# Transposed one-hots of the attention round: one VectorE operation of eight tiles, or four of two tiles each

## The chip, the cores and the metric

The kernel runs on one core of one Trainium2 chip. The metric is the device time of one launch in microseconds, from runs on the chip. Times of single instructions come from one profiled execution.

## What is computed

A graph of 6250 nodes with 128 features and 106250 edges (100000 drawn ones and one loop for each node) goes through four layers, each with a residual and a layer norm. The change lies in the second one, the attention layer. Cut to what matters:

```
h = (x @ lin_w.T).reshape(n, HEADS, HEAD_DIM)
a_src = (h * att_src).sum(-1)
a_dst = (h * att_dst).sum(-1)
logits = jax.nn.leaky_relu(a_src[src] + a_dst[dst], NEG_SLOPE)
seg_max = jax.ops.segment_max(logits, dst, num_segments=n)
e = jnp.exp(logits - seg_max[dst])
denom = jax.ops.segment_sum(e, dst, num_segments=n)
alpha = e / denom[dst]
agg = jax.ops.segment_sum(h[src] * alpha[:, :, None], dst, num_segments=n)
```

The edges are sorted by destination. The logits of the edge's own destination, `a_dst[dst]`, and of its loop are looked up by a matmul: a one-hot of the destination, turned (node by edge), against 128 rows of node logits.

## The kernel before

The edges lie in 832 tiles of 128, in 104 batches of G = 8 tiles. The attention round walks through the 104 batches. Each engine has its own program, written out by hand, with semaphores between them; no scheduler moves anything. Every engine runs the body of one batch (`slot`) four times in a loop, so a lap is four batches or 32 tiles; the first and the last batches stand outside the loop.

What each engine does for a batch:

- **POOL** gathers the rows of `table_gat` (features and source logits of each edge's source) with eight indirect DMAs, line 849, one for each tile, into a ring of four buffers (tile names `H` and `GB` in the trace). It waits for the list of indices (ACT, line 1197) and for the messages of four batches earlier (line 2319).
- **DVE** starts the slot with the running maxima of the batch (lines 2328 and 2330), which wait for PE's turned logits (line 1575); then come the differences (2307, 2309), the ends of the tiles (2336), and **`ahead`, line 2258: the turned one-hots of the next batch**, one `tensor_scalar` over 128 x 1024 bf16 elements: `LROW` holds the local destination of each edge in every partition, and it is compared with the partition's number `pidx`. Behind it on DVE stand the messages (2316 and four operations in 2319), the scans across tiles (2341 to 2352), the adding of sums (1969, 1971), more scans (2359 to 2370) with two additions for the looked-up logits (2269), and last the next batch's edge logits, `edge_sum` (line 2288), which wait for the gather of that batch, with 2295 and 2302 behind them.
- **PE** does a small matmul for the ends (1618), the eight look-up matmuls of the next batch (1585), which wait for the whole of `ahead`, the sums of an earlier batch (1599, 1600), small matmuls for maxima and scale (1626, which waits for 2344; 1629, 1630), the eight matmuls that sum the messages (1635), which wait for 2319, and then the transposes 1640 and 1575. DVE's next slot waits for 1575.
- **ACT** makes exponentials (1173, 1176), stages indices (1197), copies the looked-up logits (1192), and makes the straight one-hots (1183, 1186).
- **SP** loads the next `LROW` (line 754) when `ahead` of two batches earlier is through, and other inputs of the batch.

The constant `PIECE` is 2; the messages (2319) are already cut by it: one operation for every two tiles.

Of the kernel before, what the change touches and what calls it, by code (L numbers as in the profile page):

```python
# [22 lines left out]
ALU = mybir.AluOpType  # L23
# [3 lines left out]
P = 128  # L27
# [12 lines left out]
G = 8  # L40
# [29 lines left out]
PIECE = 2  # L70
# [12 lines left out]
def build(nc, a, out):  # L83
    ctx = ExitStack()
    with ctx:
        ctx.enter_context(nc.allow_non_contiguous_dma(reason="columns of indices and of biases, once"))

        def sb(name, shape, dt=FP32):
            return ctx.enter_context(nc.sbuf_tensor(name, shape, dt))

        def sem(name):
            return ctx.enter_context(nc.semaphore(name))
# [25 lines left out]
        pidx = sb("pidx", [P, 1])  # L118
# [82 lines left out]
        def of_tout(columns):  # L201
            free_t[0] += columns
            return TOUT[:, :, :].rearrange("p b n -> p (b n)")[:, free_t[0] - columns:free_t[0]]

        MW = of_tout(2 * G * MW_COLS).rearrange("p (b j f) -> p b j f", b=2, j=G)
        LROW = of_tout(G * P).bitcast(BF16).rearrange("p (b e) -> p b e", b=2)
        OHT = of_tout(G * P // 2).bitcast(BF16).rearrange("p (j e) -> p j e", j=G)
# [77 lines left out]
        def blocks_of(g):  # L285

            return range(4 * g, min(4 * g + 4, XBLOCKS))
# [242 lines left out]
        def n0_centered(g, n):  # L530

            return PS[:, 4 * (g % 2) + n // 2, n % 2 * (NL + P):(n % 2 + 1) * (NL + P)]
# [28 lines left out]
        chain_d, soft_d, ahead_d = sem("chain_d"), sem("soft_d"), sem("ahead_d")  # L561
# [11 lines left out]
        def at(steps, k, step="all"):  # L573

            return (k + BEFORE) * len(steps) + (steps.index(step) + 1)
# [1282 lines left out]
        def _(dve):  # L1858
# [362 lines left out]
            for g in range(GROUPS):  # L2221
# [9 lines left out]
                for n, q in enumerate(blocks):  # L2231
                    ins = dve.scalar_tensor_tensor(X[:, q * P:(q + 1) * P], n0_centered(g, n)[:, NL:], inv_root[:, q:q + 1], BC,
                                                   ALU.mult, ALU.add)
# [20 lines left out]
            def ahead(k, b, at_i):  # L2254

                dve.wait_ge(lrow_in[b], 16 * at_i)
                dve.wait_ge(look_p, at(ONE, k - 1))
                dve.tensor_scalar(OHT[:, :, :].rearrange("p j e -> p (j e)"), LROW[:, b, :], pidx[:, 0:1], None,
                                  ALU.is_equal).then_inc(ahead_d, 1)

            def look_part(k, b, n):

# [127 lines left out]
            def slot(i, c):  # L2390
# [10 lines left out]
                if now < BATCHES - 1:  # L2401
                    ahead(k + 1, 1 - b, half + 1 + b)
# [30 lines left out]
            def next_edges(k, c, at_i):  # L2433
# [3 lines left out]
                edge_or_loop(k, c % 2)  # L2437

            ahead(0, 0, 1)
            for n in (1, 2):  # L2440
                look_part(0, 0, n)
# [10 lines left out]
            for t in STEPS:  # L2452
                g = t
                if 0 <= g < GROUPS:
                    m, b = len(blocks_of(g)), g % 2
# [25 lines left out]
                if 0 <= g < GROUPS:  # L2481
# [5 lines left out]
                    for n, q in enumerate(blocks):  # L2487
                        row = X[:, q * P:(q + 1) * P]
                        ins = dve.scalar_tensor_tensor(row, ZB[g % 2][:, n, P:2 * P], inv_root[:, q:q + 1], row, ALU.mult, ALU.add)
# [349 lines left out]
```

## Time and profile before

| | |
|---|---|
| median of three runs | 5758.0 us (5751.86 to 5763.01) |
| the profiled execution, whole | 5760.18 us |
| its span, first to last instruction | 5758.3 us |
| the attention round's batches in it (line 2328) | 104, from 2470 to 3526 us |
| mean granted TensorE clock of the span | 0.839 |

Times in the trace are microseconds from the span's start. "Idle before" is the time an engine stood still ahead of an instruction, and the name behind the arrow is what ended it; "issue" means that nothing shown ended it. The duration of an instruction overlaps with the next one's on the same engine, so a chain of operations is measured from start to start.

### The profile page before, as it was taken

The numbers are of one execution on the slowest core, as the hardware profiler recorded it, in microseconds if no ns is written. First come the engines' busy times: TensorE is split into PE (matmuls) and PEld (weight loads), VectorE is DVE, ScalarE is ACT, GpSimd is POOL, SyncE is SP. The second block draws the span as 40 slices with busy tenths as digits, with TensorE's granted clock in tenths as the row PEclk, the third lists the DMA queues.
The fourth block names the chain that finished last, engine by engine and source line by source line (L and its number), as shares of the span: only waits on it lengthen the run. The fifth ranks groups of instructions, "written<-read, shape, count | busy, mean of one in ns | idle before, by whom it ended". The sixth has DMA issues, their size and how long they took to land. (4 is left out here: it accounts for less than half of the span.)

```text
span 5758.3 us, 111258 instructions
## 1 busy us (share of the span) xinstructions
PE 4169.4 (72%) x25518; PEld 3454.7 (60%) x25519; DVE 2718.9 (47%) x10515; ACT 1818.5 (32%) x5132; POOL 3986.0 (69%) x4143
## 2 busy tenths in 40 slices
PE   4688888887777787656666668566665566886896
PEld 3577777776777776545555556454544454665664
DVE  8743333433333333256666666555555545334332
ACT  0122222222222222334444444544444442001001
POOL 3177777766777777377777775577777775776777
PEclk6699999999999999755666666888888888998998
DMA  3265656652222122133333332233333324554553
GB/s 87 48 171 153 162 153 163 157 147 60 52 52 52 52 52 52 44 88 85 87 84 87 85 86 70 74 102 101 98 99 107 104 88 142 188 178 137 189 187 111
DMA packets 380789, 609.48 MB, mean 106 GB/s; under 512 B 118627, under 2 KB 288132, under 8 KB 368516
## 3 DMA queue, kind: packets, MB, share of 16 engines
q1 hardware_dynamic: 246884, 331.68, 19.2%
q0 software_dynamic: 129024, 267.91, 18.4%
q8 instruction: 241, 3.95, 0.3%
q14 instruction: 512, 4.19, 0.2%
q10 hardware_dynamic: 4128, 1.75, 0.1%
HBM read 524.61 MB, written 76.38 MB: 104 GB/s over the span
## 5 line engine op out<-in xcount | busy, mean ns | idle before, releaser
L1477 PE MATMUL PS<-ROOM 128*128 128x128 f32 x8320 | 1046.4, 282 | 101.3 <-ACT ROOM L1065 99.8
L1477 PEld LDWEIGHTS PS<-ROOM 128*128 128x128 f32 x8320 | 989.1, 196 | 159.4 <-ACT ROOM L1065 109.3
L889 POOL DMA_INDIRECT GB<-table,IDX x832 | 801.3, 963 | 352.0 <-issue 247.8
L1065 ACT COPY ROOM<-PS 128x512 f32<-128x512 f32 x1040 | 609.4, 586 | 798.8 <-PE PS L1491 793.5
L889 POOL DMA_INDIRECT GB<-in_x,IDX x416 | 403.3, 969 | 296.8 <-ACT IDX L1040 157.0
L2148 DVE TENSOR_TENSOR ROOM<-ROOM,PS 128x128 f32 x312 | 89.7, 288 | 896.4 <-PE PS L1501 875.5
L889 POOL DMA_INDIRECT ROOM<-table,IDX x416 | 404.5, 972 | 137.5 <-issue 125.4
L849 POOL DMA_INDIRECT H<-table_gat,IDX x416 | 410.7, 987 | 126.8 <-issue 115.2
L849 POOL DMA_INDIRECT GB<-table_gat,IDX x416 | 406.0, 976 | 127.6 <-issue 125.6
L889 POOL DMA_INDIRECT H<-in_x,IDX x416 | 404.6, 973 | 126.8 <-issue 126.2
L889 POOL DMA_INDIRECT H<-table,IDX x416 | 396.8, 954 | 126.8 <-issue 122.5
L861 POOL DMA_INDIRECT GB<-table,IDX x352 | 335.0, 952 | 152.0 <-issue 105.8
L1635 PE MATMUL PS<-ROOM,OH 128*128 128x144 f32 x1664 | 428.0, 450 | 1.0 <-DVE RS L2376 1.0
L1491 PE MATMUL PS<-OH,GB 128*128 128x256 f32 (+1 forms) x1664 | 340.8, 359 | 119.6 <-DMA GB<-table,IDX 75.0
L861 POOL DMA_INDIRECT ROOM<-table,IDX x352 | 334.7, 951 | 107.3 <-issue 107.0
L1635 PEld LDWEIGHTS PS<-ROOM,OH 128*128 128x128 f32 x1664 | 395.1, 330 | 2.6 <-issue 1.0
L1491 PEld LDWEIGHTS PS<-OH,GB 128*128 128x128 f32 x1664 | 283.6, 210 | 165.3 <-issue 98.4
L1034 ACT CAST ROOM<-PS 128x550 f32 x450 | 299.1, 665 | 241.1 <-PE PS L1417 185.2
L2055 DVE SCALAR_TENSOR_TENSOR H<-iota_w,key,ROOM 128x256 f32<-128x256 f32 x416 | 173.8, 482 | 320.5 <-DVEq L2128 123.8
L1491 PE MATMUL PS<-OH,H 128*128 128x256 f32 x832 | 227.0, 434 | 95.9 <-DMA H<-in_x,IDX 55.1
L1710 PE MATMUL PS<-ROOM 128*128 128x384 bf16 x1470 | 263.4, 332 | 34.3 <-DVE ROOM L2581 33.1
L1710 PE MATMUL PS<-ROOM,PACK 128*128 128x384 bf16 x1470 | 270.6, 338 | 12.6 <-issue 11.8
(418 smaller groups left out, 7769.0 us busy)
## 6 DMA issues: line engine op xcount, KB each, us to landing
H<-one_over SPq DMA_DIRECT2D x416, 128.0 KB
ROOM<-one_over SPq DMA_DIRECT2D x416, 128.0 KB
neighbours<-ROOM SPq DMA_DIRECT2D x30, 1700.0 KB
ROOM<-neighbours SPq DMA_DIRECT2D x30, 1700.0 KB
PACK<-neighbours SPq DMA_DIRECT2D x30, 1700.0 KB
ROOM<-local_row SPq DMA_DIRECT2D x104, 256.0 KB
GB<-table,IDX POOLq DMA_INDIRECT x1184
ROOM<-table,IDX POOLq DMA_INDIRECT x768
```

The source lines that it names most:

```text
L849: pool.indirect_dma_start(out=out[:, j, :], out_offset=None, in_=r.table.dram[:, :], in_offset=bass.IndirectOffsetOnAxis(ap=idx[:, j:j + 1 ...
L861: pool.indirect_dma_start(out=RING_ROWS[c][:, j * P:(j + 1) * P], out_offset=None, in_=m.table.dram[:, :], in_offset=bass.IndirectOffsetOn ...
L889: pool.indirect_dma_start(out=r.rows[c][:, j * P:(j + 1) * P], out_offset=None, in_=r.dram[:, :], in_offset=bass.IndirectOffsetOnAxis(ap=I ...
L1034: act.copy(MADE_HALVES[:, :, :, bass.ds(offsets[n] + 1, SPAN - 1)], counted_of(2)[:, :, :, 1:SPAN])
L1065: act.copy(to.rearrange("p r (j d) -> p r j d", j=r.per), of.rearrange("p (j d r) -> p r j d", j=r.per, d=NEAR))\
L1477: ins = nc.tensor.matmul(PS[:, 4, 0:P], r.near[1 - b][:, t * P:(t + 1) * P], r.weights[:, t * P:(t + 1) * P], start=t == 0, stop=t == r.re ...
L1491: ins = nc.tensor.matmul(PS[:, n, j % r.per * r.cols:(j % r.per + 1) * r.cols], r.rows[c][:, j * P:(j + 1) * P], r.hot[b][:, j * r.cols:(j ...
L1635: ins = nc.tensor.matmul(PS[:, 1 - b, 0:MW_COLS], hot(1 - b)[:, j, :], MW[:, 1 - b, j, :], start=j == 0, stop=j == G - 1)
L1710: ins = nc.tensor.matmul(PS[:, bank, 0:3 * P], NEIGH[e][:, h, 0:P], XS[:, h, :], start=h == 0, stop=h == XBLOCKS - 1)
L2055: ins = dve.scalar_tensor_tensor(to, columns, key, WINDOWS[b][:, j * r.cols:(j + 1) * r.cols], ALU.is_equal, ALU.mult, accum_out=wstage[:, ...
L2148: dve.tensor_tensor(dst, dst, PS[:, 5, 0:P], ALU.add).then_inc(added, 1)
```

## The change

`ahead` makes the one-hots in four operations of two tiles (256 columns) in place of one of eight (1024 columns). All four write the same buffer as before; the waits stand ahead of the first and the semaphore's increment is on the last, so PE, SP and DVE itself see one event for a batch, as before. The other engines' programs are the same, and so is the order of everything else on DVE.

```diff
                 dve.wait_ge(lrow_in[b], 16 * at_i)
                 dve.wait_ge(look_p, at(ONE, k - 1))
-                dve.tensor_scalar(OHT[:, :, :].rearrange("p j e -> p (j e)"), LROW[:, b, :], pidx[:, 0:1], None,
-                                  ALU.is_equal).then_inc(ahead_d, 1)
+                for j in range(0, G, PIECE):
+                    ins = dve.tensor_scalar(OHT[:, j:j + PIECE, :].rearrange("p j e -> p (j e)"), LROW[:, b, j * P:(j + PIECE) * P],
+                                            pidx[:, 0:1], None, ALU.is_equal)
+                ins.then_inc(ahead_d, 1)
```

VectorE's stream at the start of the second slot, before (H holds the logits and scans, ROOM the one-hots and messages, V the ends of the tiles):

```order
L2328 SCALAR_TENSOR_TENSOR H<-H,PS 64x128
L2330 SCALAR_TENSOR_TENSOR H<-H 64x128
L2307 TENSOR_TENSOR SPARE<-H,PS 128x128
L2309 TENSOR_TENSOR RD<-RZ 8x1
L2336 TENSOR_TENSOR V<-jmask,H 64x16
L2258 TENSOR_SCALAR ROOM<-ROOM,pidx 128x1024
L2316 TENSOR_TENSOR ROOM<-ROOM,PACK 128x8x8
L2319 TENSOR_TENSOR ROOM<-GB,ROOM 128x2x128 x4
```

The same piece of VectorE's stream now (all its lines stand two further down in the file):

```order
L2330 SCALAR_TENSOR_TENSOR H<-H,PS 64x128
L2332 SCALAR_TENSOR_TENSOR H<-H 64x128
L2309 TENSOR_TENSOR SPARE<-H,PS 128x128
L2311 TENSOR_TENSOR RD<-RZ 8x1
L2338 TENSOR_TENSOR V<-jmask,H 64x16
L2259 TENSOR_SCALAR ROOM<-ROOM,pidx 128x256 x4
L2318 TENSOR_TENSOR ROOM<-ROOM,PACK 128x8x8
L2321 TENSOR_TENSOR ROOM<-GB,ROOM 128x2x128 x4
```

Four operations stand where one stood, ahead of the messages; nothing else has another place.

## Rows read from the trace of the kernel before

**Rows 1.** The page: busy time of each engine, and the clock by slices.
```profile
PE 4169.4 (72%) x25518; PEld 3454.7 (60%) x25519; DVE 2718.9 (47%) x10515; ACT 1818.5 (32%) x5132; POOL 3986.0 (69%) x4143
...
PEclk6699999999999999755666666888888888998998
```

**Rows 2.** Groups of POOL instructions, 2590 to 3490 us (22 laps).
```profile
line engine op names shapes xcount | busy us, mean ns | idle before us <-releasers
L849 POOL DMA_INDIRECT H<-table_gat,IDX x352 | 344.3, 978 | 107.3 <-issue 96.0 <-ACT IDX L1197 10.7 <-DVE ROOM L2319 0.6
L849 POOL DMA_INDIRECT GB<-table_gat,IDX x352 | 341.7, 971 | 107.3 <-issue 106.7 <-DVE ROOM L2319 0.3 <-ACT IDX L1197 0.3
```

**Rows 3.** Line 849 alone: shortest, median and longest gather.
```profile
L849 POOL DMA_INDIRECT GB<-table_gat,IDX x416: 940/944/2718, 2451.2 to 3497.6; - x139
```

**Rows 4.** Timeline of VectorE, one lap: edge logits (2288) and slot starts (2328).
```profile
3003.01 0.41 DVE L2328 TENSOR_TENSOR_SCAN H<-H,PS 64x128 f32<-64x128 f32 x1 [4.29 <-issue]
...
3012.49 0.41 DVE L2328 TENSOR_TENSOR_SCAN H<-H,PS 64x128 f32<-64x128 f32 x1 [2.39 <-PE PS L1575]
...
3021.36 0.41 DVE L2328 TENSOR_TENSOR_SCAN H<-H,PS 64x128 f32<-64x128 f32 x1 [1.87 <-PE PS L1575]
...
3028.55 0.23 DVE L2288 TENSOR_TENSOR H<-H 128x64 f32<-128x64 f32 x1 [0.83 <-DMA H<-table_gat,IDX]
...
3030.90 0.41 DVE L2328 TENSOR_TENSOR_SCAN H<-H,PS 64x128 f32<-64x128 f32 x1 [1.40 <-PE PS L1575]
...
3038.83 0.23 DVE L2288 TENSOR_TENSOR H<-GB,H 128x64 f32<-128x64 f32 x1 [1.78 <-DMA GB<-table_gat,IDX]
...
3043.84 0.41 DVE L2328 TENSOR_TENSOR_SCAN H<-H,PS 64x128 f32<-64x128 f32 x1 [4.06 <-issue]
```

**Rows 5.** Timeline of all engines, around line 2258 in one slot.
```profile
3013.62 0.47 DVE L2258 TENSOR_SCALAR ROOM<-ROOM,pidx 128x1024 bf16<-128x1024 bf16 x1
...
3014.04 0.23 DVE L2316 TENSOR_TENSOR ROOM<-ROOM,PACK 128x64 f32<-128x64 f32 x1
...
3014.65 0.49 PE L1585 MATMUL PS<-SPARE,ROOM 128*128 128x48 bf16 x8 [0.61 <-DVE ROOM L2258]
...
3015.79 0.18 DVE L2344 TENSOR_TENSOR_SCAN ROW_B<-H,ROW_F 8x16 f32<-8x16 f32 x1
3016.00 0.15 DVE L2349 TENSOR_TENSOR RZ<-CARRY,ROW_B 8x1 f32<-8x1 f32 x1
3016.08 0.13 DVE L2350 COPY RZ<-ROW_B 8x1 f32<-8x1 f32 x1
...
3016.12 0.36 PE L1626 MATMUL PS<-ROW_B,sel 8*64 8x16 f32 x2
```

**Rows 6.** Line 2258 alone: shortest, median, longest.
```profile
L2258 DVE TENSOR_SCALAR ROOM<-ROOM,pidx x104: 467/468/661, 2466.2 to 3513.3; 128x1024 bf16<-128x1024 bf16 x104
```

**Rows 7.** Timeline of VectorE, another round: eight comparisons in a row, 512 bytes each.
```profile
5011.92 1.66 DVE L2560 TENSOR_SCALAR OH<-iota_w,local 128x128 f32<-128x128 f32 x8 [1.54 <-DVEq L2713]
```

**Rows 8.** Lines 2560 and 2383 alone: shortest, median, longest (2383: one column).
```profile
L2560 DVE TENSOR_SCALAR OH<-iota_w,local x704: 267/281/526, 4820.3 to 5701.7; 128x128 f32<-128x128 f32 x176
L2383 DVE TENSOR_SCALAR ROOM<-ROOM,RS x104: 201/214/216, 2484.2 to 3537.6; - x104
```

**Rows 9.** Timeline of VectorE and of POOL, gathers that meet line 2258.
```profile
2554.53 0.99 POOL L849 DMA_INDIRECT GB<-table_gat,IDX  x1 [0.30 <-issue]
...
3413.40 0.47 DVE L2258 TENSOR_SCALAR ROOM<-ROOM,pidx 128x1024 bf16<-128x1024 bf16 x1
...
3413.48 1.22 POOL L849 DMA_INDIRECT GB<-table_gat,IDX  x1 [0.30 <-issue]
...
3482.66 1.12 POOL L849 DMA_INDIRECT GB<-table_gat,IDX  x1 [0.30 <-issue]
```

**Rows 10.** Windows of one lap: busy time, count, granted clock (PEclk), DMA, GB/s.
```profile
3003.00:3020.00 17.00, 12.46 (x66) 10.29 (x67) 13.05 (x64) 8.97 (x27) 13.04 (x14) 0.50 0.34 75
3020.00:3024.00 4.00, 1.73 (x18) 1.25 (x16) 2.44 (x9) 0.77 (x4) 3.09 (x4) 0.93 0.56 123
```

## The prediction

> **What bounds the kernel now.** First the page: no engine is busy all the time, POOL 69% and DVE 47% [rows 1]. A share of the span says nothing about one stage, so the next view is the stage of the change, and in it the groups of the engine that may never stand still. Over 900 us of the attention round POOL issues 704 gathers, busy 344.3 + 341.7 = 686.0 us, with an idle time of 2 x 107.3 = 214.6 us ahead of them [rows 2]. That is all of the 900 us, and the idle time is 0.305 us ahead of every gather alike, whatever releaser is named: the pause between two gathers, not a wait. POOL never waits for data here. An undisturbed gather takes 0.944 us [rows 3], so 32 of them, a lap, take 32 x (0.944 + 0.305) = 39.97 us. The lap measured is 900 / 22 = 40.9 us; the missing 0.95 us are gathers that took longer (mean 0.975 us). So the round is bound by **POOL issuing gathers**, with about 0.95 us a lap of disturbance.
>
> The second view is DVE's timeline of a lap [rows 4]. It shows how much the engine that the change loads has to spare. DVE waits for gathered rows ahead of line 2288 for 0.83 us in the third slot and for 1.78 us in the fourth; in the first two slots it does not. All slot starts but the first wait for PE's transpose 1575, which stands behind the 16 message matmuls, and these behind DVE's own work of the slot: DVE and PE form one chain, at 9.48, 8.87 and 9.54 us a slot. Ahead of the first slot of each lap DVE stands for 4.1 to 4.3 us with no releaser, at the place where its loop jumps back. The chain is therefore never shorter than 3043.84 - 3003.01 = 40.83 us less the last wait, 1.78: **39.05 us a lap** if gathers cost nothing. POOL's 40.8 lies above it by 1.78 us. The wait of the third slot is covered by PE's slot time and doesn't count beside it.
>
> **The change, part by part.** *Removed:* one operation of 0.468 us [rows 6]; the next operation starts 0.42 to 0.45 us after it (3014.04 - 3013.62) [rows 5]; I take 0.43. *Added:* four of 256 bf16 columns. The nearest rows are comparisons of the same kind (a tensor against a number per partition, both in memory) over 128 f32 columns, which are the same 512 bytes: 0.281 us each [rows 8], and eight in a row take 1.66 us [rows 7], so they start every (1.66 - 0.28) / 7 = 0.197 us. Four then hold up the next operation by 4 x 0.20 = 0.80 us in place of 0.43, **0.37 us more**, and the one-hots are ready after 3 x 0.20 + 0.27 = 0.87 us in place of 0.47, **0.40 us later**. Bounds: the same with no overlap at all, 4 x 0.28 - 0.43 = 0.69 us more; and, from below, operations of one column start every 0.08 us (3016.00, 3016.08) [rows 5], to which comes a quarter of what the large one needs for its data, (0.468 - 0.214) / 4 = 0.063 us with the one-column comparison as the fixed part [rows 6, 8]: 4 x 0.145 - 0.43 = 0.15 us more. I take 0.38 for both paths, near the row that is like it in kind and bytes, and keep 0.15 and 0.69.
>
> *Who sees these 0.38 us.* Behind `ahead` on DVE everything of the slot is later, the messages first. On PE the look-up matmuls (start 0.56 us after the one-hots are ready) and, behind them, 1626 are later too; 1626 starts within 0.15 us of the end of 2344 [rows 5], so both paths move by about the same, and I count one shift of 0.38 a slot and not two. The queue of SP gets its release 0.40 us later for a load that has a batch of time. POOL waits for the messages of four batches earlier, and these are ready ten microseconds before it asks, which is why rows 2 show no such wait; nothing of POOL's own moves. Four slots: 4 x 0.38 = 1.52 us a lap. The chain becomes 39.05 + 1.52 = 40.57 us, still under the 40.83 that this lap takes. The added work is **hidden by the wait for gathered rows**, which shrinks from 1.78 to 0.26 us; if that cover were gone, it would cost 24 x 1.52 = 36 us.
>
> *What can change POOL itself.* In rows 9 a gather starts 0.08 us after line 2258 and takes 1.22 us, 0.28 more than 0.94; 3413.48 + 0.28 = 3413.76, which is 0.11 us before the comparison ends. In the loop 37 gathers meet line 2258 in this way, the first at 2554.53 and the last at 3482.66 [rows 9], some 0.1 us each, 3.8 us in all. Others are held by line 2319 and by the scans in the same way. An operation that holds for h delays a gather that falls into it by h/2 on average, and each of 32 gathers a lap falls into it with a chance of h / 10.2 for each slot. With h of 0.29 for each of 2258 and the four of 2319 (durations less 0.13), and about 0.27 for three scans and 0.1 for five small operations, the sum of h squared is 0.084 + 0.336 + 0.22 + 0.05 = 0.69, and the delay a lap is 32 x 0.69 / (2 x 10.2) = 1.08 us, against 0.95 measured. Four pieces hold for 0.1 us each with a gap between: 0.04 in place of 0.084, so 0.07 us a lap less, 24 x 0.07 = **1.7 us less**. All later operations of a slot also move against the gathers by 0.4 to 1.5 us, so the rest is drawn anew; since laps repeat nearly alike, the draw is the same 24 times. Half of it up or down, if the meeting points change, would be 0.2 us a lap or 5 us, and downward the chain stops it at 0.26 us a lap, 24 x 0.26 = 6 us.
>
> The Trainium skill has a rule for this ("SBUF — State Buffer", "Who interferes with whom"): VectorE and GpSimd share a pair of ports, and whoever issues first keeps it for the whole instruction. By it shorter instructions give the pair back sooner; the trace agrees for rows 9. It has one against the change too ("VectorE: DVE Perf Modes", "The TRN2 errata"): each instruction with its source in SBUF pays a fixed latency, so tiles should have 512 elements or more. Its formula of 58 cycles and a quarter cycle per element makes 4 x 127 - 327 = 181 ns more for four pieces (an estimate from that page), and its measured fixed part of 150 cycles would make 469 ns more; the rows lie between, and by the first figure the sum would be a chain of 39.8 us, by the second one of 40.9.
>
> **The sum.** The loop: -1.7 us for the shorter hold, 0 for 1.52 us of hidden work a lap. The eight batches outside the loop: the start waits for a load anyway and POOL's ring is four batches deep, 0; behind the last gather no `ahead` follows, 0. Together -2 us against the profiled execution, 5760.2 - 2 = 5758.2; its time is 2.2 us above the median of the runs, so **5756 us**.
>
> **The rivals.** *The port decides (faster).* If the pieces start nearly as close as the lower bound (0.15 to 0.25 us more a slot), the chain has 0.8 us of room below 40.83, and the gathers may lose half of their disturbance: -0.48 us a lap, -11.5 us, 5746 or less. For it: rows 9 and the chain of small operations. Against it: eight comparisons at 0.197 us, and only 3.8 us of all delays are line 2258's own. 8 in 100.
>
> *DVE and PE become the bound (slower).* From 1.78 / 4 = 0.445 us a slot on, the wait for gathered rows is used up and each further bit counts four times a lap. With no overlap between pieces (0.69) the lap is 39.05 + 2.76 = 41.81 us, 0.98 more, 24 x 0.98 = +23.5 us, 5781. For it: 0.38 is close to the point. Against it: every other run of like operations on this engine overlaps. The bound of 0.2% is passed from 0.56 us a slot on. 11 in 100.
>
> *The clock.* The second slot is 0.6 us shorter than its neighbours; its message matmuls run into a stretch of full clock (0.93, against 0.50 before it) [rows 10]. Should the later matmuls miss it, the chain is 40.57 + 0.6 = 41.2 us, +0.34 a lap, +8 us, 5764. 4 in 100, within the 0.2%.
>
> *The code.* The loop's body is twelve instructions longer, and DVE already stands 4.1 to 4.3 us at each jump back [rows 4]. If a second such stop came up in the lap, it would be 40.57 + 4.1 = 44.7, +3.8 a lap, +92 us, 5848. The Trainium skill tells of that stop as a fetch of a page of code after a taken branch ("Runtime: NRT & Kernel Launch", "Instruction fetch mechanics"). For it: the stop is there. Against it: there is none inside the four slots now. 3 in 100.
>
> **How the numbers follow.** The forecast, hidden work and slightly less disturbance, has 74 in 100, and its own range is 5749 to 5765. About 0.2%, 11.5 us, is what a measurement of this kernel can tell from no change. Faster by more: 0.08, the first rival. Slower by more: 0.11 + 0.03 = 0.14. Within: 0.74 + 0.04 = 0.78. The range from 5746 to 5770 leaves out half of the first two rivals and the last one, and thin ends of the forecast.
>
> **What would show it.** Four operations of some 0.27 us that start every 0.2 us; 2316 some 0.37 us later behind 2336; the wait of line 2288 in the fourth slot down from 1.78 to 0.3 us; POOL still with 0.305 us ahead of every gather and a mean of 0.965 to 0.98 us for one. The argument is wrong if that wait is gone and POOL shows waits for line 2319 or for its indices, or if DVE stands still at a second place of the lap; if POOL's mean stays but the time moves, the cause lies outside the round.

## The result, and the profile after

The changed kernel takes 5865.97 us (median of four runs, 5858.07 to 5876.2) against 5758.76 us, a ratio of 1.0189 with a 95% interval of 1.0172 to 1.0206: **slower by 107 us**, where 5756 us was forecast. Its profiled execution has a span of 5856.2 us against 5758.3, so 97.9 us of the loss can be looked for in the traces.

The first view is the page of each kernel. First the kernel before, its groups of gathers:

```profile
L849 POOL DMA_INDIRECT H<-table_gat,IDX x416 | 410.7, 987 | 126.8 <-issue 115.2
L849 POOL DMA_INDIRECT GB<-table_gat,IDX x416 | 406.0, 976 | 127.6 <-issue 125.6
```

The page of the changed kernel, its engines and the same groups:

```profile
PE 4159.3 (71%) x25518; PEld 3444.8 (59%) x25519; DVE 2752.1 (47%) x10827; ACT 1820.9 (31%) x5132; POOL 4086.0 (70%) x4143
...
L849 POOL DMA_INDIRECT H<-table_gat,IDX x416 | 474.2, 1140 | 126.8 <-issue 124.0
L849 POOL DMA_INDIRECT GB<-table_gat,IDX x416 | 440.3, 1058 | 127.6 <-issue 118.2
```

VectorE's busy time grew by 33 us, POOL's by 100 [rows 1]. The 832 gathers of the attention round took 474.2 + 440.3 = 914.5 us in place of 816.7, **97.8 us more, which is the whole loss**; their idle time, 126.8 + 127.6, is the same to a tenth. So the profile shows no place where POOL waits longer for anything. It does the same work, and each gather lasts 118 ns longer on average. From the first gather's start to the last one's it is 1166.8 us in place of 1069.0; the stretches ahead of and behind the round did not change.

The same in the loop, the groups of POOL from 2590 to 3490 us (against [rows 2]):

```profile
L849 POOL DMA_INDIRECT H<-table_gat,IDX x320 | 364.2, 1138 | 97.5 <-issue 95.1 <-ACT IDX L1197 2.1 <-DVE ROOM L2321 0.3
L849 POOL DMA_INDIRECT GB<-table_gat,IDX x323 | 341.2, 1056 | 98.4 <-issue 91.7 <-ACT IDX L1197 6.4 <-DVE ROOM L2321 0.3
```

That is 643 gathers instead of 704, with a mean of 705.4 / 643 = 1.097 us; the pause is still 195.9 / 643 = 0.305 us. POOL is the bound as before; a lap is now 32 x 1.402 = 44.9 us.

What VectorE does at the start of a slot is as forecast. Line 2259 alone, shortest, median and longest:

```profile
L2259 DVE TENSOR_SCALAR ROOM<-ROOM,pidx x416: 267/268/468, 2470.8 to 3615.6; 128x256 bf16<-128x256 bf16 x139
```

VectorE's timeline around the pieces in one slot (start, duration, engine, line, operation):

```profile
3012.05 0.86 DVE L2259 TENSOR_SCALAR ROOM<-ROOM,pidx 128x256 bf16<-128x256 bf16 x4
3012.83 0.21 DVE L2318 TENSOR_TENSOR ROOM<-ROOM,PACK 128x64 f32<-128x64 f32 x1
3012.97 1.41 DVE L2321 TENSOR_TENSOR ROOM<-H,ROOM 128x256 f32<-128x256 f32 x4
```

POOL's timeline at the same time:

```profile
3013.46 1.74 POOL L849 DMA_INDIRECT GB<-table_gat,IDX  x1 [0.30 <-issue]
3015.50 0.94 POOL L849 DMA_INDIRECT H<-table_gat,IDX  x1 [0.30 <-issue]
```

A piece takes 0.268 us, four of them 0.86 us, and the next operation starts 0.78 us after the first. The gather that starts in the second of the four message operations takes 1.74 us, 0.80 more than the undisturbed 0.94. That brings its release, worked out as start plus excess, to 3013.46 + 0.80 = 3014.26 (its *excess* is what it takes beyond the undisturbed 0.944 us), which is 0.12 us before the *last* of the four ends (3012.97 + 1.41 = 3014.38). In the kernel before, a gather that came in the same way was let in at the end of the one operation that it met. VectorE's timeline there:

```profile
3004.13 0.47 DVE L2258 TENSOR_SCALAR ROOM<-ROOM,pidx 128x1024 bf16<-128x1024 bf16 x1
3004.58 0.23 DVE L2316 TENSOR_TENSOR ROOM<-ROOM,PACK 128x64 f32<-128x64 f32 x1
3004.73 1.43 DVE L2319 TENSOR_TENSOR ROOM<-H,ROOM 128x256 f32<-128x256 f32 x4
```

And POOL's, still of the kernel before:

```profile
3005.10 1.20 POOL L849 DMA_INDIRECT GB<-table_gat,IDX  x1 [0.30 <-issue]
```

Start plus excess is 3005.36, some 0.13 us before the second message operation ends; two more followed it without a gap, and they held nothing. I worked this out for every gather of both traces. Start plus excess falls close to "end of some VectorE operation less 0.12 to 0.13 us" (0.19 us for the scans) for nearly all. "Held by" counts the VectorE operations from the one that the gather met to the one at whose end it was let in:

```
                        before            after
sum of all excess       31.9 us           129.7 us
held by one operation   171:  23.1 us     111:  16.0 us
held by 2 to 5 in a row   3:   2.6 us      70:  61.6 us
held by 6 or more         3:   5.4 us      24:  48.5 us
not attributed            6:   0.4 us      11:   3.2 us
over 600 ns               6 gathers       74 gathers, 101.5 us
```

In the changed kernel 110 us of excess are gathers held by a **row of operations instead of one**, against 8.0 us before; that difference is the loss. The longest ones met the pieces: the gather at 3031.51 started as the pieces did and was let in when the messages ended, nine operations later. VectorE's timeline in that slot of the changed kernel:

```profile
3031.54 0.86 DVE L2259 TENSOR_SCALAR ROOM<-ROOM,pidx 128x256 bf16<-128x256 bf16 x4
3032.32 0.21 DVE L2318 TENSOR_TENSOR ROOM<-ROOM,PACK 128x64 f32<-128x64 f32 x1
3032.46 1.41 DVE L2321 TENSOR_TENSOR ROOM<-GB,ROOM 128x256 f32<-128x256 f32 x4
```

POOL's:

```profile
3031.51 3.18 POOL L849 DMA_INDIRECT H<-table_gat,IDX  x1 [0.30 <-issue]
```

**What differs ahead of such a row.** The message operations are the same in both kernels and start 0.335 us apart in both. Two things of the moment at which they start differ. VectorE's sequencer, which reads its program and does the waiting, can be ahead of the engine. How far it has come shows in the register load of line 596, which the sequencer does itself and which stands in the stream just behind the four messages. That load in the slot above of the kernel before (line 596 alone; its start stands twice, to a tenth):

```profile
L596 DVEq TENSOR_LOAD <-meta x1: 750/750/750, 3004.9 to 3004.9; - x1
```

And in the slot of the changed kernel:

```profile
L596 DVEq TENSOR_LOAD <-meta x1: 756/756/756, 3012.8 to 3012.8; - x1
```

Before, the load starts 0.14 us *after* the first message operation (3004.73); after, 0.2 us *before* it (3012.97): the sequencer had handed over all four and gone on. What holds the sequencer back is the wait for the exponentials that stands ahead of line 2318 (2316 before); they come from line 1173 of ScalarE. Its timeline in the slot of the kernel before:

```profile
3004.09 0.31 ACT L1173 ACTIVATE ROOM<-SPARE 128x128 f32<-128x128 f32 x1 [5.04 <-DVE SPARE L2307]
```

And of the changed kernel:

```profile
3012.00 0.31 ACT L1173 ACTIVATE ROOM<-SPARE 128x128 f32<-128x128 f32 x1 [5.14 <-DVE SPARE L2309]
```

They end about 0.27 us after the comparison's start in both kernels (3004.40 against 3004.13, 3012.31 against 3012.05). One large comparison then has 0.2 us left to run, four pieces have 0.6. In the first case the sequencer is released just in time, in the second with time to spare. The other difference is that line 2318 starts 0.07 us before the operation ahead of it has ended, where line 2316 did so by 0.02 us in the slot shown, and that it is shorter. Its duration (shortest, median, longest) in the kernel before, as line 2316:

```profile
L2316 DVE TENSOR_TENSOR ROOM<-ROOM,PACK x104: 204/224/300, 2477.5 to 3535.3; 128x64 f32<-128x64 f32 x104
```

And in the changed kernel, as line 2318:

```profile
L2318 DVE TENSOR_TENSOR ROOM<-ROOM,PACK x104: 200/206/228, 2482.9 to 3637.1; 128x64 f32<-128x64 f32 x104
```

The median of this operation, 224 or 206 ns, turned out to be the quickest sign of which case a kernel is in.

Lastly VectorE's waits in the loop (engine, line, what it waited for: sum, times, longest), of the kernel before:

```profile
DVE H L2288 <- DMA GB<-table_gat,IDX: 38.8, 22, 2.3
DVE H L2288 <- DMA H<-table_gat,IDX: 20.1, 23, 1.5
```

And of the changed kernel:

```profile
DVE H L2290 <- DMA H<-table_gat,IDX: 93.1, 39, 3.6
DVE H L2330 <- issue: 72.0, 20, 4.2
...
DVE H L2290 <- DMA GB<-table_gat,IDX: 58.3, 24, 3.6
```

It waits for gathered rows for 151.4 us in place of 58.9. The added work did not use the wait up; POOL became slower and made it longer. The stop without a releaser still comes once a lap, 3.6 us on average, and at no second place.

### The profile page after: what moved, and what is told of

It is laid out like the page before. It is cut to its first block and busy times, and to the rows that moved or that the text cites. A ratio compares the mean times of both kernels' runs of the same rounds, so it can differ in the third digit from the quotient of the medians.

```text
span 5856.2 us, 111570 instructions
## 1 busy us (share of the span) xinstructions
PE 4159.3 (71%) x25518; PEld 3444.8 (59%) x25519; DVE 2752.1 (47%) x10827; ACT 1820.9 (31%) x5132; POOL 4086.0 (70%) x4143
## 5 line engine op out<-in xcount | busy, mean ns | idle before, releaser
L849 POOL DMA_INDIRECT H<-table_gat,IDX x416 | 474.2, 1140 | 126.8 <-issue 124.0
L849 POOL DMA_INDIRECT GB<-table_gat,IDX x416 | 440.3, 1058 | 127.6 <-issue 118.2
L889 POOL DMA_INDIRECT H<-in_x,IDX x416 | 404.7, 973 | 126.8 <-issue 126.5
L889 POOL DMA_INDIRECT H<-table,IDX x416 | 396.4, 953 | 126.8 <-issue 121.3
```

What stands on the lines that cost most here:

```text
L849: pool.indirect_dma_start(out=out[:, j, :], out_offset=None, in_=r.table.dram[:, :], in_offset=bass.IndirectOffsetOnAxis(ap=idx[:, j:j + 1 ...
L889: pool.indirect_dma_start(out=r.rows[c][:, j * P:(j + 1) * P], out_offset=None, in_=r.dram[:, :], in_offset=bass.IndirectOffsetOnAxis(ap=I ...
```

## The experiments

The theory: **VectorE operations that the sequencer hands over ahead of their start keep GpSimd out from the first to the last, as if they were one instruction; operations that it hands over one at a time let GpSimd in at each end.** The rivals: the messages' later start by itself (they meet the gathers elsewhere, or VectorE and TensorE become the bound), and the pieces by themselves. The results together; "line 2316" is the first message operation under whatever number it has:

```
kernel                                ratio to before [95%]    excess  >600 ns  line 2316
                                                               of all           median
before                                                         31.9 us    6      224 ns
after                                 1.0189 [1.0172, 1.0206]  129.7     74      206
e1  after, wait for pieces            0.9996 [0.9986, 1.0005]   29.7      1      225
e2  before, wait for comparison       0.9981 [0.9971, 0.9991]   25.1      0      226
e2b the same kernel, more runs        0.9994 [0.9985, 1.0003]   25.1      0      226
e3  before, filler behind comparison  1.0086 [1.0069, 1.0103]   84.9     64      203
e7  before, filler earlier            1.0018 [1.0009, 1.0028]   41.5      6      225
e5  before, wait between messages     1.0050 [1.0033, 1.0067]   21.4      1      225
e4  two pieces of four                1.0088 [1.0070, 1.0106]   91.0     50      206
e8  four pieces, wait on third        1.0021 [1.0012, 1.0030]   37.2      7      225
e9  two pieces, wait on first         0.9991 [0.9981, 1.0000]   29.0      4      225
e10 messages as one operation         1.0045 [1.0029, 1.0060]   55.3     25      224
```

**e1: the changed kernel, with nothing but a wait for the last piece ahead of the messages.** VectorE does more waiting and the messages start later still.

```diff
                 if now < BATCHES - 1:
                     ahead(k + 1, 1 - b, half + 1 + b)
+                    ahead_own(k + 1, "oht")
                 if 1 <= now <= BATCHES:
                     messages(k - 1, (c + 3) % 4)
```

> The changed kernel, and behind the four pieces VectorE waits for their own end before it goes on to the messages. Theory A (one long hold): back-to-back operations keep the shared ports from POOL as one block; the pieces start so close that they join with 2318 and 2321 into one block of 2.2 us, and a gather that meets it takes up to 3.2 us. The wait cuts the block in two (some 0.7 and 1.4 us), so gathers over 2.5 us vanish and the time falls most of the way back, to 5760 to 5790. Theory B (lateness): the 0.37 us by which everything of the slot is later moves the gathers into the messages, whatever stands ahead of them; with the wait the slot is later still, and the time stays at 5840 or more.

Measured: 5756.85 us, ratio 0.9996 (0.9986 to 1.0005). The whole loss is gone. VectorE's timeline of a slot:

```profile
3011.33 0.86 DVE L2259 TENSOR_SCALAR ROOM<-ROOM,pidx 128x256 bf16<-128x256 bf16 x4
3012.45 0.23 DVE L2318 TENSOR_TENSOR ROOM<-ROOM,PACK 128x64 f32<-128x64 f32 x1 [0.26 <-DVE ROOM L2259]
```

POOL's groups from 2590 to 3490 us:

```profile
L849 POOL DMA_INDIRECT H<-table_gat,IDX x352 | 352.1, 1000 | 107.3 <-issue 102.1 <-DVE ROOM L2321 4.9 <-ACT IDX L1197 0.3
L849 POOL DMA_INDIRECT GB<-table_gat,IDX x351 | 334.0, 951 | 107.0 <-issue 100.9 <-ACT IDX L1197 6.1
```

Line 2318 starts 1.12 us after the first piece, 0.34 later than in the changed kernel, and yet the gathers are back at 686.1 / 703 = 0.976 us. That speaks against both rivals at once: the pieces are all there and the messages are later than ever. It came out 3 us below the 5760 to 5790 of the theory. The pieces by themselves still form a short row here: 25 gathers were held across two to four of them, 9.5 us in all, and the longest excess is 0.75 us. The run also shows the cover of the prediction at work: in this trace VectorE has no wait for gathered rows left in the loop, and the time is that of the kernel before.

**e3: the kernel before, with a filler behind the comparison.** Two reductions of a constant into a tile that nobody reads keep VectorE busy for as long as the extra pieces do. No one-hot is cut.

```diff
+        filler = sb("filler", [P, 2])
...
                 if now < BATCHES - 1:
                     ahead(k + 1, 1 - b, half + 1 + b)
+                    for n in range(2):
+                        dve.tensor_reduce(filler[:, n:n + 1], iota_f[:, :], AXIS.X, ALU.add)
```

> The kernel before, with the one whole comparison, and behind it two reductions of 128 x 128 f32 to one column (some 0.4 us together, one input, not among the operations that met gathers in the trace). They make the rest of the slot as late as the change does, but neither cut the comparison nor join it to the messages. Theory A: within 15 us of 5758. Theory B: the lateness alone does it, 5840 or more.

Measured: 5809.12 us, ratio 1.0086 (1.0069 to 1.0103), 64 gathers over 600 ns. VectorE's timeline in one slot (lines stand one higher):

```profile
2641.22 0.47 DVE L2259 TENSOR_SCALAR ROOM<-ROOM,pidx 128x1024 bf16<-128x1024 bf16 x1
2641.62 0.46 DVE L2405 TENSOR_REDUCE filler<-iota_w 128x1 f32<-128x128 f32 x2
2642.01 0.20 DVE L2317 TENSOR_TENSOR ROOM<-ROOM,PACK 128x64 f32<-128x64 f32 x1
2642.14 1.41 DVE L2320 TENSOR_TENSOR ROOM<-H,ROOM 128x256 f32<-128x256 f32 x4
```

POOL's timeline beside it:

```profile
2642.82 1.56 POOL L850 DMA_INDIRECT GB<-table_gat,IDX  x1 [0.31 <-issue]
```

The gather came in the third message operation and was let in at the end of the fourth, no sooner. So the loss comes without the changed comparison: these two reductions, which keep VectorE busy between the exponentials and the messages, are enough. The expectation was **missed** on both sides: the theory as I had it then, with the cut comparison as the cause, gave 5758 within 15 us, and lateness alone 5840 or more.

The loss is half that of the changed kernel, since the rows are shorter. The longest excess is 1.31 us, against 2.24, and the part "6 or more" (48.5 us) is missing. The reductions themselves hold nothing. VectorE's timeline in another slot:

```profile
2909.76 0.46 DVE L2405 TENSOR_REDUCE filler<-iota_w 128x1 f32<-128x128 f32 x2
```

POOL's:

```profile
2909.80 0.94 POOL L850 DMA_INDIRECT H<-table_gat,IDX  x1 [0.30 <-issue]
```

This gather started 0.04 us into the first reduction and was not held at all, in a slot in which the register load stands 0.21 us ahead of the first message. The same goes for all 28 that started within a reduction and 0.13 us or more before its end: their excess is at most 0.01 us. Gathers that met the comparison were let in at its end. So a row is not just anything that was handed over ahead: here it began behind the reductions.

**e7: the same filler, but ahead of the differences**, from which the exponentials are made, so that they come later too (the kernels of e7, e4, e8 and e2b ran beside a kernel before of 5764.23 us).

```diff
+                if now < BATCHES - 1:
+                    for n in range(2):
+                        dve.tensor_reduce(filler[:, n:n + 1], iota_f[:, :], AXIS.X, ALU.add)
                 if 1 <= now <= BATCHES:
                     differences(k - 1, 1 - b)
```

> The kernel before, with the same two reductions (0.4 us) as in the run with them behind the comparison, but now ahead of the differences (2307), so that the exponentials, and with them the wait ahead of the messages, are as late as all the rest. Theory C (the lead): a run of message operations keeps POOL out as one block only where the sequencer has issued all of it before its first operation begins; the traces so far show the register load behind the messages 0.2 to 0.4 us ahead of the first message operation where a block is kept, and 0.02 us or more behind it where POOL gets in between. Here the wait for the exponentials holds the sequencer back as before, so no block: 5750 to 5775. Theory B (lateness): the slot is 0.4 us later just the same, so 5800 or more.

Measured: 5774.23 us, ratio 1.0018 (1.0009 to 1.0028), 10 us. The same two operations in the same slot cost 10 us here and 49 us in e3; the place alone decides. The sequencer is held by the exponentials as before, and only 6 gathers pass 600 ns. These 10 us, too, are in gathers that lasted longer (41.5 us of excess against 31.9) and not in a wait: 15 gathers were held across short rows that end with the comparison, lines 2308, 2310, 2337 and 2259, for 7.7 us in all. Together with e1 this bounds what up to 0.7 us of later work a slot costs in this round: nothing to 10 us.

**e2 and e2b: the kernel before, with the wait of e1**, the same kernel twice, first with few runs and then with more.

```diff
                 if now < BATCHES - 1:
                     ahead(k + 1, 1 - b, half + 1 + b)
+                    ahead_own(k + 1, "oht")
```

> The kernel before with the same wait behind the whole comparison, 0.1 to 0.2 us later. Theory A: the comparison already lets POOL in before the messages, so nothing changes: 5750 to 5770. Theory B: between before and after, 5770 to 5830.

> The kernel before with the wait behind the whole comparison once more, with more rounds, since one round gave a ratio of 0.9981 (0.9971 to 0.9991). Theory C: the few blocks of the first and last batches are gone (8 us in the trace of before) and the loop is as it was, so 0.1 to 0.3% faster, 5742 to 5752.

Measured: 5747.03 us, 0.9981 (0.9971 to 0.9991), then 5762.63 us, 0.9994 (0.9985 to 1.0003). The six gathers over 600 ns (8.0 us of excess, in the first and last batches) are gone from both traces, and the excess falls from 31.9 to 25.1 us. But the gain of the first eight runs was not confirmed by eleven more, and the 5742 to 5752 us expected of these were **missed**: no difference that can be measured.

**e5: the kernel before, with a wait for its own result between the messages.** VectorE stops after each of the first three, so that a row of four can't exist.

```diff
-        SOFT_D = ("diff", "rd", "own", "m", "rs", "sums", "aux")
+        SOFT_D = ("diff", "rd", "own", "m1", "m2", "m3", "m", "rs", "sums", "aux")
...
+                    if j + PIECE < G:
+                        ins.then_inc(soft_d, 1)
+                        soft_own(k, "m%d" % (j // PIECE + 1))
```

> The kernel before, with VectorE waiting for the end of each of the first three message operations (line 2319) before the next, some 0.1 us each. Theory A: no block is longer than 0.4 us, so no gather takes over 1.4 us anywhere, also in the first and last batches (six did before, 8 us in all), and the disturbance of a lap falls from 0.95 to 0.5 us or so; VectorE's chain grows by 4 x 0.35 = 1.4 us a lap and stays hidden: 5740 to 5755. Theory B, in which only the meeting points count: anything from 5750 to 5840, with long gathers still there.

Measured: 5790.66 us, ratio 1.0050 (1.0033 to 1.0067). The excess is the smallest of all, 21.4 us, and yet the kernel is 31 us slower, where 5740 to 5755 were expected: a **miss**, and another bound. VectorE's timeline in one slot:

```profile
3020.91 1.79 DVE L2319 TENSOR_TENSOR ROOM<-H,ROOM 128x256 f32<-128x256 f32 x4
3023.30 0.23 DVE L2344 TENSOR_TENSOR_SCAN ROW_F<-H,CARRY,PS 8x16 f32<-8x16 f32 x1 [0.60 <-issue]
```

Its two largest waits in the loop:

```profile
DVE H L2331 <- PE PS L1575: 172.0, 75, 3.3
DVE ROW_F L2344 <- issue: 49.5, 84, 0.6
```

One of POOL's two groups in the loop:

```profile
L849 POOL DMA_INDIRECT H<-table_gat,IDX x342 | 329.6, 964 | 129.5 <-issue 107.7 <-DVE ROOM L2319 20.6 <-ACT IDX L1197 1.2
```

The messages take 0.36 us longer, and the register load of line 596, which before ran beside them, now comes behind them and holds up line 2344 by 0.59 us. That is about 1 us a slot. VectorE waits for TensorE (172.0 us, against 125.3 before and 70.4 in the changed kernel) and no longer for gathered rows, and POOL waits 20.6 us for messages in this group, against 0.6 in [rows 2]; over the whole round POOL is idle for 288 us in place of 254. The rival "VectorE and TensorE become the bound" exists, and this is what it looks like. In the changed kernel POOL's idle time is that of before, and VectorE waits longer for gathered rows.

**e4: two pieces of four tiles.** The extra time on VectorE is about a fifth of that of four pieces (the next operation starts 0.52 us after the first, against 0.45 in the kernel before and 0.78).

```diff
-                for j in range(0, G, PIECE):
-                    ins = dve.tensor_scalar(OHT[:, j:j + PIECE, :] ... LROW[:, b, j * P:(j + PIECE) * P],
+                for j in range(0, G, 4):
+                    ins = dve.tensor_scalar(OHT[:, j:j + 4, :] ... LROW[:, b, j * P:(j + 4) * P],
```

> Two pieces of four tiles: the next operation is held up by some 0.53 us, against 0.43 (whole) and 0.80 (four pieces). Theory C: the exponentials are ready some 0.4 us after the comparison starts, so the sequencer gets a lead of 0.1 us, less than the 0.2 us seen with kept blocks: some blocks at most, 5760 to 5800. If the number of pieces alone counted: half of the loss, 5810.

Measured: 5816.47 us, ratio 1.0088 (1.0070 to 1.0106), 50 gathers over 600 ns. I had expected so small a lead of the sequencer to be harmless, and **missed**. VectorE's timeline in one slot:

```profile
2608.37 0.59 DVE L2259 TENSOR_SCALAR ROOM<-ROOM,pidx 128x512 bf16<-128x512 bf16 x2
2608.89 0.21 DVE L2318 TENSOR_TENSOR ROOM<-ROOM,PACK 128x64 f32<-128x64 f32 x1
2609.03 1.41 DVE L2321 TENSOR_TENSOR ROOM<-GB,ROOM 128x256 f32<-128x256 f32 x4
```

POOL's:

```profile
2609.50 1.77 POOL L849 DMA_INDIRECT H<-table_gat,IDX  x1 [0.30 <-issue]
```

The row holds as in the changed kernel. The register load starts 0.02 to 0.07 us behind the first message in most of these slots, only 0.07 to 0.12 us sooner than in the kernel before, so a small difference in the lead is enough. The time is also close to the 5810 us that were expected if the number of pieces alone counted; e9, with the same two pieces, rules that out.

**e8: four pieces, and a wait for the third.** The last piece still runs when the sequencer goes on, and VectorE hardly stands still.

```diff
-        AHEAD_D = ("oht", "look1", "look2", "sum", "edge", "any")
+        AHEAD_D = ("oht3", "oht", "look1", "look2", "sum", "edge", "any")
...
+                    if j == 2 * PIECE:
+                        ins.then_inc(ahead_d, 1)
...
                     ahead(k + 1, 1 - b, half + 1 + b)
+                    ahead_own(k + 1, "oht3")
```

> The changed kernel, with VectorE waiting for the end of the third piece (not the last) before it issues the messages: the sequencer is held back, the engine itself hardly is (it still has the fourth piece to do). Theory C: the messages are issued as they begin, no block is kept, 5745 to 5765. A variant of A, in which an empty moment of the engine is what lets POOL in: there is none here, so 5840 or more.

Measured: 5775.45 us, ratio 1.0021 (1.0012 to 1.0030), 10 us above the range of the theory and 65 below that of the rival. Of 45 gathers that started in the first three messages and were held for 0.05 us or more, 43 were let in at the end of the operation that they met. So it takes no pause as long as that of e1 (0.26 us): nine tenths of the loss are gone. The 7 gathers over 600 ns (11.0 us, the longest excess 2.26 us) all lie in the first and last batches, outside the loop; four of them met the pieces and were held to the end of the messages, across the point of the wait. In the slots of these four the register load comes 0.20 us ahead of the first message, while in the loop it comes 0.13 us behind it. Of the 11 us that remain, the traces show 5.9 between the first and the last gather; the rest is not explained.

**e9: two pieces, and a wait for the first.** The edit of e8 on the kernel of e4.

```diff
-        AHEAD_D = ("oht", "look1", "look2", "sum", "edge", "any")
+        AHEAD_D = ("oht1", "oht", "look1", "look2", "sum", "edge", "any")
...
+                    if j == 0:
+                        ins.then_inc(ahead_d, 1)
...
+                    ahead_own(k + 1, "oht1")
```

> The changed kernel with two pieces of four tiles, and VectorE waits for the end of the first piece before it issues the four message operations. Without that wait the same two pieces gave 5816.5 us, with 50 gathers over 600 ns (64.1 us of excess); the run of messages had then been issued 0.04 to 0.09 us before its first operation began. Theory of the sequencer's lead (a run of message operations that was issued before its first operation starts keeps GpSimd out until the whole run ends; one that is issued operation by operation lets it in at each operation's end): the wait makes the messages be issued later than the second piece's start, so no such lead remains in most slots; fewer than 15 gathers over 600 ns, excess 25 to 45 us, 5750 to 5775 us. Rival, that two back-to-back pieces and what follows them leave GpSimd no opening whatever the sequencer did: the pieces and the messages follow each other as closely as before, so 40 gathers or more over 600 ns, 5800 to 5825 us.

Measured: 5753.09 us, ratio 0.9991 (0.9981 to 1.0000), 4 gathers over 600 ns, all outside the loop, excess 29.0 us, as the theory had it. VectorE's timeline in one slot:

```profile
3190.12 0.62 DVE L2259 TENSOR_SCALAR ROOM<-ROOM,pidx 128x512 bf16<-128x512 bf16 x2
3190.76 0.22 DVE L2320 TENSOR_TENSOR ROOM<-ROOM,PACK 128x64 f32<-128x64 f32 x1
3190.90 1.42 DVE L2323 TENSOR_TENSOR ROOM<-H,ROOM 128x256 f32<-128x256 f32 x4
```

POOL's:

```profile
3191.31 1.15 POOL L849 DMA_INDIRECT GB<-table_gat,IDX  x1 [0.30 <-issue]
```

Line 2320 starts 0.64 us after the first piece, 0.12 later than in e4, with no pause to speak of (0.02 us). The same phase of a gather, 0.41 to 0.47 us into the messages, gives 1.77 us in e4 and 1.15 us here.

**e10: the kernel before, with the four messages as one operation.** A row that holds should act like one long instruction; here is one.

```diff
-                for j in range(0, G, PIECE):
-                    tiles = slice(j, j + PIECE)
+                for j in range(0, G, G):
+                    tiles = slice(j, j + G)
...
-                                            MW[:, b, tiles, P:P + HEADS].unsqueeze(3).to_broadcast([P, PIECE, HEADS, HD]), ALU.mult)
+                                            MW[:, b, tiles, P:P + HEADS].unsqueeze(3).to_broadcast([P, G, HEADS, HD]), ALU.mult)
```

> The kernel before, with the four message operations of 256 columns each made one operation of 1024 columns, so that VectorE reads two tensors of SBUF for about 1.1 us without an end in between. Theory that a held run of four acts on GpSimd as one long operation: gathers that meet it are held up to 1.2 us more; with one such run for about eleven gathers and a hit in a third of the slots, some 60 to 100 gathers over 600 ns, an excess of 80 to 130 us against 31.9 us in the kernel before, 5800 to 5860 us. Rival, that the loss of the changed kernel comes from the pieces themselves and not from the length for which the messages keep the ports: excess stays under 45 us, 5750 to 5770 us.

Measured: 5782.33 us, ratio 1.0045 (1.0029 to 1.0060), 25 gathers over 600 ns, excess 55.3 us. VectorE's timeline in one slot:

```profile
2783.64 1.22 DVE L2319 TENSOR_TENSOR ROOM<-GB,ROOM 128x1024 f32<-128x1024 f32 x1
```

POOL's:

```profile
2784.19 1.48 POOL L849 DMA_INDIRECT H<-table_gat,IDX  x1 [0.30 <-issue]
```

Start plus excess is 2784.73, 0.13 us before the operation's end, as for a held row. The mechanism is that of the changed kernel; its size was **missed**: 80 to 130 us of excess and 5800 to 5860 us were expected. The one operation is 1.22 us long, while a held row with the pieces in it reaches 2.2 us, and the gathers happened to come late in it (95 met it, 35.4 us, a mean of 0.37 us each). VectorE does the same work in less time here, and the kernel is slower.

## Why the prediction was wrong

**The step that failed is "What can change POOL itself".** It took each VectorE operation for an obstacle of its own, so that a hold h costs h squared over two and cutting one operation into four must help: 1.7 us less. The sum of squares agreed with the trace of before (1.08 us a lap against 0.95), but only because in that trace each operation did release POOL at its end. The runs show that to be a condition of the moment. Nine operations of 0.2 to 0.4 us, the pieces and the messages, were one obstacle of up to 2.2 us in the changed kernel. By the same sum, the four messages as one obstacle of 1.41 - 0.13 = 1.28 us put 1.64 in the place of 0.336, which is 32 x 1.30 / 20.4 = 2.0 us more a lap; pieces and messages as one of 2.2 us put 4.84 in the place of 0.42, 6.9 us more. The 97.8 / 24 = 4.1 us a lap that were lost lie between: the rule that I used had the loss in it, if I had asked when neighbours count as one. "Half of it up or down" was no bound for this. None of the rivals had the mechanism.

The Trainium skill ("SBUF — State Buffer", "Who interferes with whom") says of VectorE's two-port modes that whoever issues first has the shared ports for the whole instruction, and that an operation with two inputs in SBUF contends with a GpSimd instruction that reads. The trace of e10 agrees with the second: an operation of 1.22 us with two inputs kept a gather out until 0.13 us before its end. Taken instruction by instruction, no gather that meets a message would be held for more than about 0.3 us; the trace of after has 0.80 us at 3013.46, and the measurement decides.

The other steps, in their order. *What bounds the kernel*: right, POOL issuing gathers, before and after. *The pieces' cost*: 0.20 us apart and 0.27 us long was forecast, 0.195 to 0.197 and 0.268 measured; the next operation 0.78 us behind the first against 0.80. *Hidden*: right as far as it went. e1 has 0.34 us a slot on top of the change and loses nothing. By my sum its chain would be 39.05 + 4 x 0.67 = 41.7 us, and its laps are 40.97, as before (40.98): the chain is less stiff than I had it, and the rival "VectorE and TensorE become the bound" was overrated. It begins somewhere between the 0.67 us a slot of e1, which cost nothing, and the 0.95 of e5. *The wait for gathered rows* went from 58.9 to 151.4 us and not down, since POOL itself was late; the sign that I had named for the forecast, a POOL mean of 0.965 to 0.98 us, failed with 1.097. *The code*: no second stop, as forecast. *The clock*: nothing points to it. The granted TensorE clock of the round is 0.61 in both traces, and the loss is in POOL's durations to 0.1 us.

What could have been read beforehand: the trace of the kernel before holds six gathers over 600 ns, all in the first and last batches, up to 1.86 us ([rows 3] shows a longest one of 2.718 us against a median of 0.944). I took them for odd ends. By the same reading they are held rows; in all six the register load starts 0.20 to 0.25 us ahead of the messages.

**What stays open.** Take the ten traces other than e5 and e10, and in them the 541 gathers that started within the first three messages and were held for 0.05 us or more. Where the register load started 0.125 us or more after the first message, 292 of 292 were held by no more than the operation that they met. Where it started less than 0.10 us after it, or before it, 182 were held to the end of the row and 60 were not (7 lie between the two, none held to the end). Most of the 60 share a second sign: by how much line 2316 and its like overlap the operation ahead of them. At 60 to 74 ns of overlap 176 of the 179 gathers were held to the end, at 75 to 80 ns 52 of 53 were not. What these few nanoseconds stand for the trace does not show, so early handing over is not the whole condition. Nor is it told apart from the way in which the row begins: where the sequencer hands over one at a time, line 2316 overlaps the operation ahead by less than 60 ns, or starts behind its end, in 282 of the 292. Nor does the theory say why the reductions of e3, handed over ahead like the rest, hold nothing. That the resource is the shared pair of ports was not tested by itself, though e10 fits it.

## What to carry to other kernels

Where GpSimd issues indirect gathers without pause and is the bound, look at what VectorE has queued and not only at how long one of its operations is: a row of operations that start back to back can cost like a single one of their total length. A wait that holds VectorE's sequencer until just before the row can be worth more than the time that it takes (in e1 it took back 107 us for a pause of 0.26 us a slot), and a change that makes such a wait come true early, like more work ahead of it, can take this away without touching the row. In the profile, compare the shortest and the longest of the bound engine's own instructions, not only its waits.

## What the runs showed of the hardware

- VectorE operations in a row held an indirect gather of GpSimd for up to 2.24 us across nine instructions (2.26 us in e8). Handed over one at a time, the messages hold it for 0.3 us at most, and it comes in 0.12 to 0.13 us before an operation's recorded end. In e4 the sequencer was only 0.07 to 0.12 us earlier than in the kernel before, and 49 of its gathers were held to the end of the messages.
- Two `TENSOR_REDUCE` operations of 128x128 f32 to one column held no gather, also where the messages behind them did (28 gathers, e3).
- A VectorE multiplication of two tensors in SBUF (`TENSOR_TENSOR`, 1.22 us) kept 95 gathers that met it out until 0.12 to 0.13 us before its end (e10).
- The held time appears as duration of the gather (0.94 us becomes 3.18), never as idle time: the pause between two gathers was 0.305 us in every kernel in which POOL was the bound.
- Line 2316 and its like are recorded some 20 ns shorter in the kernels with held rows, where they overlap the operation ahead by about 0.07 us (median of 203 to 206 ns in after, e3 and e4, against 224 to 226 in the others).
- Four operations of 256 bf16 columns started 0.195 us apart and took 0.268 us each, one of 1024 took 0.468 us.
